# Five of the nine low one-hot rows of each counting step move from VectorE to GpSimd

## The chip, the cores and the metric

The kernel runs on one core of a Trainium2 chip. The metric is device time in microseconds, the median of several executions.

## The reference

A graph of 50,000 nodes (64 features each) and 50,000 edges, sorted by destination, goes through seven passes: a convolution, a mean aggregation, a GATv2 attention layer with four heads and batch norm, and three typed graph convolutions, each behind a layer norm and added to its input. All of them need to know how many edges leave and enter each node, which is what the first stage counts:

```python
deg = jnp.maximum(jax.ops.segment_sum(jnp.ones(dst.shape, jnp.float32), dst, num_segments=50000), 1.0)
deg_isqrt = deg ** (-0.5)
...
deg_s = jax.ops.segment_sum(ones, s, num_segments=n)
deg_r = jax.ops.segment_sum(ones, r, num_segments=n)
...
cnt = jax.ops.segment_sum(jnp.ones((edge_attr.shape[0],), x.dtype), dst0, num_segments=n)
```

## The kernel before

The program is a chain of stages, each a block in which the five engines run lists of their own, and no stage starts before all engines have left the one ahead. `prepare` (lines 131 to 403) comes first. It loads indices, x and weights, counts degrees, and makes the norms from the counts. Small planning stages follow, then the layers, which fill the rest of the run.

**The counting loop** is a histogram made by matrix products. The 392 tiles of 128 edges (50,176 slots) are taken seven at a time (`HS`), so there are 56 steps, and the loop's body holds two of them, one for each half `s` of the double-buffered tensors `hi` and `lo`. Each index is split in a low byte and a high part (`dig`, in the memory of `alpha`). For each of the seven tiles `t` of a step and both index lists `j` (0 source, 1 destination), two one-hot rows of bf16 are built on 128 partitions: `hi` with 196 columns and `lo` with 256. TensorE multiplies the two and adds up in `bank4` and `bank5`: 7 x 2 x 2 = 28 matmuls of 256 columns a step (line 390).

Three engines work on a step:

- **VectorE** (lines 322 to 332) compares `iota_b` (0..255) with the digit: one `tensor_scalar` per row, 14 `hi` rows and 9 `lo` rows (all seven of `j` = 1, and tiles 5 and 6 of `j` = 0), then adds one to `oh`.
- **ScalarE** (lines 240 to 250) makes the other five `lo` rows (`SPLIT` = 5, `j` = 0) as relu(1 - |iota - digit|): a negated copy of seven digits `low` (line 243), five `Abs` (line 246), and one `Relu` over 1280 columns (line 250), which adds one to `oh_low`.
- **TensorE** waits for `oh` and `oh_low` of the step, multiplies, and adds one to `counted`.

Before they write a half again, VectorE and ScalarE wait until `counted` shows that the step two back is done; ScalarE takes that wait only ahead of line 250. **GpSimd** makes three `iota` fills at the start of the stage (lines 261 to 263) and has nothing more in it. SyncE's queue brings x in, and copies edge attributes in HBM (line 208) behind the loop's first part. The rows of the loop lie on `iota_b`, `dig`, `hi` and `lo`, all in SBUF.

After the loop VectorE copies the counts from PSUM (line 338), TensorE turns them (line 402), and the norms are made (lines 348 to 361).

Of the kernel before, what the change touches and what calls it, by code (L numbers as in the profile page):

```python
# [4 lines left out]
P = 128  # L5
# [3 lines left out]
HS = 7  # L9
# [4 lines left out]
WT = HS + 1  # L14
WR = WT * P
SPLIT = 5
BAND = 2
FRONT = P
LN_EPS = 1e-5
# [6 lines left out]
def build_gnn(nc, a, out):  # L26
    f32, bf16, i32 = mybir.dt.float32, mybir.dt.bfloat16, mybir.dt.int32
    ALU, ACT, AX = mybir.AluOpType, mybir.ActivationFunctionType, mybir.AxisListType
# [7 lines left out]
    NS = T // HS  # L36
# [37 lines left out]
    with ctx:  # L74
# [18 lines left out]
        node_id = sb("node_id", [P, P])  # L93
        edge_id = sb("edge_id", [P, max(NS * HS * BAND, 3 * HF)])
        rel_w = sb("rel_w", [P, 2, NS * WT])
# [35 lines left out]
        def prepare():  # L131
            with nc.cleanup_on_exit(), ExitStack() as c, nc.Block() as block:
                tb = lambda name, shape, dt=f32: c.enter_context(nc.sbuf_tensor(name, shape, dt))
                sm = lambda name: nc.alloc_semaphore("pre_" + name)
# [10 lines left out]
                dig_i, dig = digits(amax).bitcast(i32), digits(alpha)  # L145
                iota_i = tb("iota_i", [P, 256], i32); iota_b = tb("iota_b", [P, 256], bf16)
                hi = tb("hi", [P, 2, 2, HS, HI], bf16)
                lo = tb("lo", [P, 2, 2, HS, 256], bf16)
# [8 lines left out]
                iotas = sm("iotas"); turned = sm("turned"); taken = sm("taken"); w_in = sm("w_in")  # L157
                x_in = sm("x_in"); oh = sm("oh"); counted = sm("counted"); hist_ok = sm("hist_ok")
                cleared = sm("cleared"); hist_t = sm("hist_t"); sq_in = sm("sq_in"); sq_out = sm("sq_out")
                oh_low = sm("oh_low"); low = tb("low", [P, 2, HS])  # L160
                dist = tb("dist", [P, SPLIT, 256], bf16)
                tails = sm("tails"); types_out = sm("types_out"); summed = sm("summed"); w_n = sm("w_n")
                x_parts = [(k * FULL // 4, (k + 1) * FULL // 4) for k in range(4)]
# [51 lines left out]
                def _(act):  # L215
# [24 lines left out]
                    def body(i, first):  # L240
                        for s in range(2):

                            A.mul(low[:, s, :], dig[:, 1, bass.ds(i * BODY + s * HS, HS)], -1.0)
                            act.drain()
                            for t in range(SPLIT):
                                A.activation(dist[:, t, :], iota_b[:, :], ACT.Abs, bias=low[:, s, t:t + 1], scale=1.0)
                            act.drain()
                            if not first:
                                act.wait_ge(counted, 2 * i + s - 1)
                            A.activation(lo[:, s, 0, 0:SPLIT, :], dist[:, :, :], ACT.Relu, bias=onesP[:, 0:1], scale=-1.0).then_inc(oh_low, 1)  # L250
                    body(0, True)
# [7 lines left out]
                @block.gpsimd  # L259
                def _(pool):  # L260
                    nc.gpsimd.iota(row_i[:, :], pattern=[[1, P]], base=0, channel_multiplier=0)
                    nc.gpsimd.iota(col_i[:, :], pattern=[[0, 1]], base=0, channel_multiplier=1)
                    nc.gpsimd.iota(iota_i[:, :], pattern=[[1, 256]], base=0, channel_multiplier=0).then_inc(iotas, 1)

                @block.vector
                def _(dve):
# [55 lines left out]
                    def body(i, first):  # L322
                        for s in range(2):
                            if not first:
                                dve.wait_ge(counted, 2 * i + s - 1)
                            for t in range(HS):
                                for j in range(2):
                                    g = i * BODY + s * HS + t
                                    ins = v.tensor_scalar(hi[:, s, j, t, :], iota_b[:, 0:HI], dig[:, 2 * j, bass.ds(g, 1)], None, ALU.is_equal)
                                    if j == 1 or t >= SPLIT:  # L330
                                        ins = v.tensor_scalar(lo[:, s, j, t, :], iota_b[:, :], dig[:, 2 * j + 1, bass.ds(g, 1)], None, ALU.is_equal)
                            ins.then_inc(oh, 1)
                    body(0, True)
                    with v.Fori(1, GI) as i:
                        body(i, False)
                    dve.wait_ge(summed, 1)
                    for j in range(2):
                        ins = v.tensor_copy(hist[:, j, :], bank[4 + j][0:R, :])
# [31 lines left out]
                @block.tensor  # L370
                def _(pe):
                    pe.wait_ge(ident_ok, 1)
                    pe.wait_ge(floats, 1)
                    pe.wait_ge(put, 1)
                    for j in range(4):
                        for b in range(NBLK):
                            ins = nc.tensor.transpose(bank[j][:, b * R:(b + 1) * R], rows[:, j, b, :], ident[0:R, 0:R])
                    ins.then_inc(turned, 1)
                    pe.wait_ge(cleared, 1)
                    for j in range(2):  # L380
                        nc.tensor.matmul(bank[4 + j][0:R, :], zb[:, 0:R], zb[:, :], start=True, stop=False)

                    def body(i, first):
                        for s in range(2):
                            pe.wait_ge(oh, 2 * i + s + 1)
                            pe.wait_ge(oh_low, 2 * i + s + 1)
                            for t in range(HS):
                                for j in range(2):
                                    for k in range(2):
                                        ins = nc.tensor.matmul(bank[4 + j][0:R, k * 256:(k + 1) * 256], hi[:, s, j, t, k * R:(k + 1) * R],  # L390
                                                               lo[:, s, j, t, :], start=False, stop=False)
                            ins.then_inc(counted, 1)
                    with nc.tensor.Fori(0, GI) as i:
                        body(i, False)
                    for j in range(2):
                        ins = nc.tensor.matmul(bank[4 + j][0:R, :], zb[:, 0:R], zb[:, :], start=False, stop=True)
                    ins.then_inc(summed, 1)
                    pe.wait_ge(hist_ok, 1)
                    for j in range(2):
                        for k in range(2):  # L400
                            for half in range(2):
                                ins = nc.tensor.transpose(bank[j][:, (2 * k + half) * R:(2 * k + half + 1) * R],
                                                          hist[:, j, k * 256 + half * P:k * 256 + (half + 1) * P], ident[0:R, 0:R])
                    ins.then_inc(hist_t, 1)
# [1200 lines left out]
        def plan():  # L1605
            with nc.cleanup_on_exit(), ExitStack() as c, nc.Block() as block:
# [36 lines left out]
                def _(dve):  # L1643
# [35 lines left out]
                    v.tensor_tensor(ahead[:, :], tot[:, 0:NS], slots(tile_at[:, 0, :])[:, :, 0], ALU.subtract)  # L1679
                    v.tensor_scalar(late[:, :], late[:, :], float(BAND * P), None, ALU.is_gt)  # L1680
                    v.tensor_scalar(early[:, :], early[:, :], float(FRONT), None, ALU.is_gt)
# [17 lines left out]
        def window_numbers():  # L1699

            with nc.cleanup_on_exit(), ExitStack() as c, nc.Block() as block:
# [26 lines left out]
                def _(dve):  # L1728
# [8 lines left out]
                    v.drain()  # L1737
                    ids = edge_id[:, 0:NS * HS * BAND].rearrange("p (n t q) -> p n t q", t=HS, q=BAND)
                    at = tile_at[:, :].rearrange("p (n t) -> p n t", t=HS)
                    for q in range(BAND):  # L1740
                        v.tensor_tensor(ids[:, :, :, q], winT[:, :, q:q + HS], at, ALU.subtract)
# [155 lines left out]
        def layer(tag, kind, table_in, table_out, k=0):  # L1897
            with nc.cleanup_on_exit(), ExitStack() as c, nc.Block() as block:
# [8 lines left out]
                msg = tb("msg", [P, 2, WT, M])  # L1907
                S = tb("S", [P, 2, BAND * HS, P])
                own = None if conv else tb("own", [P, 2, HS + 1, 2 * F if sage else F])
# [87 lines left out]
                def _(pe):  # L1997
                    def sums(j, s, first):
# [12 lines left out]
                        for b, (t0, t1) in enumerate(CH):  # L2011
                            for t in range(t0, t1):
                                col = slice((t - t0) * P, (t - t0 + 1) * P)
                                to = bank[2 * s + b][0:M, col]
                                qs = range(BAND)
                                if sage:
# [560 lines left out]
        def batch_norm(tag):  # L2577
            with nc.cleanup_on_exit(), ExitStack() as c, nc.Block() as block:
# [68 lines left out]
                def _(dve):  # L2647
# [23 lines left out]
                    body(GI - 1, False, True)  # L2671

        prepare()
        attention_weights()
        plan()
# [56 lines left out]
```

## Time and profile before

| what | value |
|---|---|
| median of 3 runs | 6772.4 us (6759.16 to 6790.24) |
| profiled execution, its own time | 6746.68 us |
| its span, first to last instruction | 6745.1 us |
| mean granted TensorE clock | 0.759 of full speed |
| PE busy | 4393.0 us (65%) |
| DVE busy | 3539.0 us (52%) |
| ACT busy | 2200.7 us (33%) |
| POOL busy | 2825.2 us (42%) |

The counting loop lies between 31 and 277 us of the span. The busy times above are sums over stages that are bound by different engines, so they say little about this loop; it is read from its own stretch. Duration and spacing differ: on VectorE one instruction's record overlaps the next one's, so the time that an instruction costs its engine is the distance between two starts, not the duration in its record.

### The profile page before, as it was taken

How to read it: one execution, taken by the hardware profiler on the slowest of the kernel's cores; microseconds unless marked ns; L12 is line 12 of the kernel's file. 1: busy time of each engine (PE TensorE's matmuls, PEld its weight loads, DVE VectorE, ACT ScalarE, POOL GpSimd, SP SyncE). 2: the span in 40 equal slices, each digit the busy share in tenths (PEclk: the TensorE clock that was granted, in tenths of full speed). 3: DMA queues.
4: the chain of work that ended last, by engine and by line, in shares of the span. 5: the costliest groups of instructions: out<-in, count | busy, mean ns of one | idle time of the engine just before them, and what ended most of it. 6: DMA issues, size and time to landing. Idle time of an engine off the chain costs nothing. (4 is left out here: it accounts for less than half of the span.)

```text
span 6745.1 us, 89039 instructions
## 1 busy us (share of the span) xinstructions
PE 4393.0 (65%) x26272; PEld 3765.7 (56%) x26272; DVE 3539.0 (52%) x9258; ACT 2200.7 (33%) x5554; POOL 2825.2 (42%) x2867
## 2 busy tenths in 40 slices
PE   6502565546666787776659999415777477757777
PEld 5402555536655454554447777315777467656677
DVE  8862555624444565665579999762323223323333
ACT  6572544513333232232225444551111111111111
POOL 0014554255543677776500000025554455545553
PEclk9855666667777787887779999656777677777777
DMA  6033666645654222222222222343444344434444
GB/s 171 6 68 82 145 144 141 134 92 126 127 116 104 63 66 66 66 68 62 50 42 55 53 52 55 81 95 80 97 93 98 69 92 96 92 81 90 96 93 91
DMA packets 1695961, 589.73 MB, mean 87 GB/s; under 512 B 1606839, under 2 KB 1626102, under 8 KB 1695498
## 3 DMA queue, kind: packets, MB, share of 16 engines
q1 hardware_dynamic: 1189958, 380.24, 25.6%
q10 hardware_dynamic: 416196, 116.81, 7.7%
q0 software_dynamic: 89600, 90.32, 6.7%
q8 instruction: 80, 1.31, 0.1%
q14 instruction: 127, 1.04, 0.0%
HBM read 378.26 MB, written 222.06 MB: 89 GB/s over the span
## 5 line engine op out<-in xcount | busy, mean ns | idle before, releaser
L1944 POOL DMA_INDIRECT early<-node_g,src_w x1176 | 1141.7, 971 | 1036.1 <-DMA edge_h<-early 583.8
L1944 POOL DMA_INDIRECT l1ring<-node_g,src_w x392 | 373.5, 953 | 444.7 <-DMA edge_h<-l1ring 243.0
L1091 POOL DMA_INDIRECT fscat<-node_g,early x392 | 439.2, 1120 | 263.5 <-issue 114.3
L1206 DVE TENSOR_TENSOR fslz<-bank,fsy 128x512 f32<-128x512 f32 x448 | 267.0, 621 | 497.6 <-issue 290.9
L1944 POOL DMA_INDIRECT l0ring<-node_g,src_w x392 | 375.4, 958 | 346.2 <-DMA edge_h<-l0ring 219.8
L2604 POOL COPY x_sb<-fbxn 128x448 f32 x56 | 31.5, 562 | 1140.0 <-DVE fbxn L2663 1140.0
L1093 POOL DMA_INDIRECT fscat<-node_g,early x392 | 433.9, 1107 | 128.2 <-issue 128.2
L1182 ACT ACTIVATE fsy<-bank 128x512 f32<-128x512 f32 x448 | 242.3, 544 | 737.1 <-remote 234.6
L2021 PE MATMUL bank<-l0S,l0msg 128*128 128x128 f32 x1568 | 297.8, 366 | 146.2 <-issue 97.6
L1141 PE MATMUL bank<-Wlr,fscatT 128*128 128x256 f32 x784 | 273.1, 433 | 171.6 <-ACT fscatT L1173 147.6
L2021 PE MATMUL bank<-l1S,l1msg 128*64 128x128 f32 x1568 | 300.6, 312 | 124.8 <-issue 124.2
L2021 PEld LDWEIGHTS bank<-l0S,l0msg 128*128 128x128 f32 x1568 | 279.8, 276 | 158.9 <-issue 153.6
L2390 PE MATMUL bank<-early,faS 128*128 128x256 f32 x1568 | 357.1, 386 | 0.0
L2390 PEld LDWEIGHTS bank<-early,faS 128*128 128x128 f32 x1568 | 296.1, 192 | 73.9 <-issue 35.2
L2021 PE MATMUL bank<-l5S,l5msg 128*128 128x128 f32 x1568 | 248.7, 323 | 123.2 <-issue 71.1
L2021 PE MATMUL bank<-l3S,l3msg 128*128 128x128 f32 x1568 | 245.0, 321 | 124.0 <-issue 79.2
L2021 PE MATMUL bank<-l4S,l4msg 128*128 128x128 f32 x1568 | 240.4, 316 | 114.5 <-issue 69.1
L2542 DVE SCALAR_TENSOR_TENSOR faagg<-bank,early,famine 128x64 f32<-128x64 f32 x1568 | 305.8, 276 | 6.2 <-ACT famine L2443 1.6
L2021 PEld LDWEIGHTS bank<-l1S,l1msg 128*64 128x64 f32 x1568 | 223.9, 161 | 150.7 <-issue 150.6
L2021 PEld LDWEIGHTS bank<-l5S,l5msg 128*128 128x128 f32 x1568 | 233.8, 236 | 130.0 <-issue 129.4
L2021 PEld LDWEIGHTS bank<-l3S,l3msg 128*128 128x128 f32 x1568 | 231.8, 234 | 128.1 <-issue 128.1
L2021 PEld LDWEIGHTS bank<-l4S,l4msg 128*128 128x128 f32 x1568 | 226.5, 229 | 120.7 <-issue 120.4
(328 smaller groups left out, 11365.2 us busy)
## 6 DMA issues: line engine op xcount, KB each, us to landing
node_g<-amax ACTq DMA_DIRECT2D x168, 224.0 KB
edge_h<-early SPq DMA_DIRECT2D x168, 224.0 KB
early<-node_g,src_w POOLq DMA_INDIRECT x1176
l0msg<-edge_a SPq DMA_DIRECT2D x56, 256.0 KB
l0msg<-edge_h SPq DMA_DIRECT2D x56, 256.0 KB
l1msg<-edge_h SPq DMA_DIRECT2D x56, 256.0 KB
alpha<-edge_h SPq DMA_DIRECT2D x56, 256.0 KB
l3win<-edge_h SPq DMA_DIRECT2D x56, 256.0 KB
```

The costliest lines, as they stand in the source:

```text
L1091: pool.indirect_dma_start(out=cat[:, s, t, 0:F], out_offset=None, in_=node_g, in_offset=bass.IndirectOffsetOnAxis(ap=src_i[:, col], axis=0 ...
L1093: pool.indirect_dma_start(out=cat[:, s, t, F:2 * F], out_offset=None, in_=node_g, in_offset=bass.IndirectOffsetOnAxis(ap=dst_i[:, col], ax ...
L1141: nc.tensor.matmul(to, catT[:, t * P:(t + 1) * P], Wlr[:, :], start=True, stop=False)
L1182: A.activation(y[:, g % 2, 0:t1 - t0, :], z_bank(g)[:, 0:(t1 - t0) * HF].rearrange("p (t c) -> p t c", c=HF), ACT.Copy, scale=SLOPE).then_ ...
L1206: v.tensor_tensor(lz[:, kind, t0:t1, :], z_bank(g)[:, 0:(t1 - t0) * HF].rearrange("p (t c) -> p t c", c=HF), y[:, g % 2, 0:t1 - t0, :], AL ...
L1944: pool.indirect_dma_start(out=ring[:, n % RING, t, :], out_offset=None, in_=table_in, in_offset=bass.IndirectOffsetOnAxis(ap=src_w[:, n * ...
L2021: ins = nc.tensor.matmul(to, msg[:, s, t + q, :], S[:, s, BAND * t + q, :], start=(q == 0 and not sage), stop=(q == BAND - 1))
L2390: ins = nc.tensor.matmul(bank[b][:, (t - t0) * HF:(t - t0 + 1) * HF], S[:, s, BAND * t + q, :], M[:, s, t + q, 0:HF], start=(q == 0), stop ...
L2542: ins = v.scalar_tensor_tensor(agg[:, s, t, h, :], bank[b][:, lo:lo + F], cc[:, 0, t, h:h + 1], mine[:, t, h, :], ALU.mult, ALU.add)
L2604: nc.gpsimd.tensor_copy(x_sb[:, bass.ds(j * BODY + s * HS, HS), :], xn[:, s, :, :]).then_inc(x_kept[s], 1)
```

## The change

GpSimd gets a list of its own in the counting loop: after the digits are there (`cleared`) it builds, for each of the 56 steps, the `lo` rows of `j` = 1 for tiles 0 to 4 (`POOLED` = 5), with the instruction that VectorE used. From step 2 on it first waits for `counted`, as the others do. It adds one to a new semaphore `oh_pool` per step, and TensorE waits for that too. VectorE builds `lo` rows only for tiles 5 and 6 of either `j`: 14 `hi` and 4 `lo` rows a step.

```diff
+POOLED = 5
...
+                    pool.wait_ge(cleared, 1)
+
+                    for n in range(NS):
+                        if n >= 2:
+                            pool.wait_ge(counted, n - 1)
+                        for t in range(POOLED):
+                            ins = nc.gpsimd.tensor_scalar(lo[:, n % 2, 1, t, :], iota_b[:, :], dig[:, 3, n * HS + t:n * HS + t + 1], None, ALU.is_equal)
+                        ins.then_inc(oh_pool, 1)
...
-                                    if j == 1 or t >= SPLIT:
+                                    if t >= (SPLIT, POOLED)[j]:
                                         ins = v.tensor_scalar(lo[:, s, j, t, :], iota_b[:, :], dig[:, 2 * j + 1, bass.ds(g, 1)], None, ALU.is_equal)
...
                             pe.wait_ge(oh_low, 2 * i + s + 1)
+                            pe.wait_ge(oh_pool, 2 * i + s + 1)
```

GpSimd's list in `prepare`, before. The rows are the three fills; what follows them is the end of the stage:

```order
L261 IOTA row_i 128x128
L262 IOTA col_i 128x1
L263 IOTA iota_i 128x256
L132 UNCONDITIONAL_BRANCH
L132 ISA [waits barrier_Pool_Activation_PE_DVE_SP_gather]
```

The same place now (nine lines further down in the file). `pre_cleared` and `pre_counted` are the semaphores `cleared` and `counted`; the last row shown is that of step 3, and the pattern goes on to step 55:

```order
L262 IOTA row_i 128x128
L263 IOTA col_i 128x1
L264 IOTA iota_i 128x256
L271 TENSOR_SCALAR lo<-iota_b,alpha 128x256 [waits pre_cleared]
L271 TENSOR_SCALAR lo<-iota_b,alpha 128x256 x9
L271 TENSOR_SCALAR lo<-iota_b,alpha 128x256 [waits pre_counted]
L271 TENSOR_SCALAR lo<-iota_b,alpha 128x256 x4
L271 TENSOR_SCALAR lo<-iota_b,alpha 128x256 [waits pre_counted]
L271 TENSOR_SCALAR lo<-iota_b,alpha 128x256 x4
```

GpSimd's list has gained 280 instructions, written out without a loop, with a wait ahead of each five.

VectorE's list at the start of a half step in the loop, before: a `hi` row of either `j` and then a `lo` row, tile by tile. The `ISA` rows compute the address of the digit:

```order
L329 ISA [waits pre_counted]
L329 TENSOR_SCALAR hi<-iota_b,alpha 128x196
L329 ISA
L329 TENSOR_SCALAR hi<-iota_b,alpha 128x196
L331 ISA
L331 TENSOR_SCALAR lo<-iota_b,alpha 128x256
L329 ISA
L329 TENSOR_SCALAR hi<-iota_b,alpha 128x196
L329 ISA
L329 TENSOR_SCALAR hi<-iota_b,alpha 128x196
L331 ISA
L331 TENSOR_SCALAR lo<-iota_b,alpha 128x256
```

And now, where the first ten rows of the step are `hi` rows and `lo` rows come with the last two tiles (here its last rows, up to the next step's wait):

```order
L338 TENSOR_SCALAR hi<-iota_b,alpha 128x196
L340 ISA
L340 TENSOR_SCALAR lo<-iota_b,alpha 128x256
L338 ISA
L338 TENSOR_SCALAR hi<-iota_b,alpha 128x196
L340 ISA
L340 TENSOR_SCALAR lo<-iota_b,alpha 128x256
L338 ISA [waits pre_counted]
```

Five `lo` rows and their address instructions have left each step of VectorE; the wait stands where it stood.

## Rows read from the trace of the kernel before

**Rows 1.** Page, busy tenths in 40 slices of 168.6 us.

```profile
PE   6502565546666787776659999415777477757777
...
DVE  8862555624444565665579999762323223323333
...
POOL 0014554255543677776500000025554455545553
PEclk9855666667777787887779999656777677777777
```

**Rows 2.** Busy time by stretch: length, then each engine's busy us.

```profile
core 0: us, PE busy (x) PEld busy (x) DVE busy (x) ACT busy (x) POOL busy (x), PEclk, DMA share, GB/s
...
31.00:277.00 246.00, 186.43 (x1572) 171.25 (x1572) 240.29 (x1289) 201.14 (x393) 0.00 (x0) 1.00 0.38 98
...
200.00:277.00 77.00, 59.09 (x506) 54.30 (x506) 73.22 (x394) 58.99 (x114) 0.00 (x0) 1.00 0.00 0
```

**Rows 3.** Groups of instructions between 31 and 277 us, shapes apart.

```profile
L329 DVE TENSOR_SCALAR hi<-iota_b,alpha 128x196 bf16<-128x196 bf16 x784 | 234.3, 527 | 1.9 <-PE bank L390 1.8
L331 DVE TENSOR_SCALAR lo<-iota_b,alpha 128x256 bf16<-128x256 bf16 x504 | 218.4, 543 | 0.0
L390 PE MATMUL bank<-lo,hi 128*98 128x256 bf16 x1568 | 184.9, 276 | 59.3 <-DVE lo L331 59.3
...
L246 ACT ACTIVATE dist<-iota_b,low 128x256 bf16<-128x256 bf16 x280 | 117.9, 497 | 3.8
L250 ACT ACTIVATE lo<-dist,onesP 128x1280 bf16<-128x1280 bf16 x56 | 76.3, 1363 | 34.4 <-PE bank L390 34.2
```

**Rows 4.** Line 329: duration ns min/median/max, first and last start.

```profile
L329 DVE TENSOR_SCALAR hi<-iota_b,alpha x784: 266/531/773, 31.1 to 272.1; 128x196 bf16<-128x196 bf16 x196
```

**Rows 5.** Timeline of VectorE inside one step: start us, us, instruction.

```profile
207.19 0.65 DVE L329 TENSOR_SCALAR hi<-iota_b,alpha 128x196 bf16<-128x196 bf16 x1
207.37 0.66 DVE L331 TENSOR_SCALAR lo<-iota_b,alpha 128x256 bf16<-128x256 bf16 x1
207.57 0.65 DVE L329 TENSOR_SCALAR hi<-iota_b,alpha 128x196 bf16<-128x196 bf16 x1
```

**Rows 6.** Timeline of TensorE, two steps of the counting loop.

```profile
204.55 3.26 PE L390 MATMUL bank<-lo,hi 128*98 128x256 bf16 x28 [1.02 <-DVE lo L331]
208.84 3.26 PE L390 MATMUL bank<-lo,hi 128*98 128x256 bf16 x28 [1.03 <-DVE lo L331]
```

**Rows 7.** Timeline of ScalarE, an early step and a late one.

```profile
42.73 0.20 ACT L243 ACTIVATE low<-alpha 128x7 f32 x1
...
45.17 1.36 ACT L250 ACTIVATE lo<-dist,onesP 128x1280 bf16<-128x1280 bf16 x1
46.44 0.19 ACT L243 ACTIVATE low<-alpha 128x7 f32 x1
...
207.85 1.36 ACT L250 ACTIVATE lo<-dist,onesP 128x1280 bf16<-128x1280 bf16 x1 [0.64 <-PE bank L390]
```

**Rows 8.** GpSimd's groups of instructions, whole run.

```profile
L2604 POOL COPY x_sb<-fbxn 128x448 f32 x56 | 31.5, 562 | 1140.0 <-DVE fbxn L2663 1140.0
...
L1629 POOL IOTA pl_tile_i<- 128x392 int32 x1 | 0.5, 455 | 308.1 <-POOLq L2250 308.1
...
L263 POOL IOTA iota_i<- 128x256 int32 x1 | 0.3, 334 | 0.0
```

**Rows 9.** Line 1091's durations; timelines of GpSimd and VectorE near 2630 us.

```profile
L1091 POOL DMA_INDIRECT fscat<-node_g,early x392: 942/947/2778, 2139.3 to 3335.7; - x196
...
2632.04 2.50 POOL L1091 DMA_INDIRECT fscat<-node_g,early  x1 [0.30 <-issue]
...
2631.69 2.02 DVE L1213 TENSOR_TENSOR fslz<-fslz,attb 128x1792 f32<-128x1792 f32 x1
```

**Rows 10.** TensorE's 28 matmuls of line 2021 at two speeds, chain that ended last.

```profile
6108.56 5.60 PE bank L2021 x28
6117.68 3.18 PE bank L2021 x28
```

More of the change, by code:

```diff
@@ L159, in prepare @@
                 cleared = sm("cleared"); hist_t = sm("hist_t"); sq_in = sm("sq_in"); sq_out = sm("sq_out")
-                oh_low = sm("oh_low"); low = tb("low", [P, 2, HS])
+                oh_low = sm("oh_low"); oh_pool = sm("oh_pool"); low = tb("low", [P, 2, HS])
                 dist = tb("dist", [P, SPLIT, 256], bf16)
```

## The prediction

> **What bounds the kernel now.** I looked first for where the change lies in the whole run. The page's slices show the counting loop in the first two of forty: VectorE 8 tenths busy, GpSimd idle, TensorE's granted clock near full [rows 1]. The stretch table says it more sharply. Between 31 and 277 us GpSimd does nothing, the granted clock is 1.00 (TensorE's upper level, 2.4 GHz), and by the last 77 us the DMA share has fallen to 0.00 [rows 2]. So the loop is not covered by a transfer, and the next stage starts only when it is over: a microsecond off or on the loop is a microsecond of the run. It is about 246 us of 6745, which caps what any edit here can bring.
>
> Next, who sets the pace inside the loop. The groups name it: TensorE was idle 59.3 us ahead of its matmuls, all of it until a VectorE `lo` row, and ScalarE 34.2 us ahead of its `Relu`, until TensorE. VectorE was idle 1.9 us in 784 instructions [rows 3]. VectorE is the bound, and the two others wait for it.
>
> What a step costs on each engine is read from distances between starts. Line 329's records grow from 266 to 773 ns in the course of the loop [rows 4] while their distance stays the same, so the duration isn't the price. On VectorE a `hi` row takes 0.18 us to the next start and a `lo` row 0.20 [rows 5]. TensorE's batches start 4.29 us apart and are 3.26 long [rows 6]. 14 x 0.18 = 2.52; the other 1.77 are nine `lo` rows at 0.197. ScalarE, on an early step where it had no wait, went from `low` to `low` in 3.71 us [rows 7]. So a step is **VectorE 4.29, ScalarE 3.71, TensorE 3.26, GpSimd 0**, and there are 56.
>
> **The change, part by part.**
>
> *Removed from VectorE:* five `lo` rows a step, 5 x 0.197 = 0.98 us, their address instructions included, since those lie inside the distances. VectorE alone would need 4.29 - 0.98 = 3.30 (3.31 before rounding). The next engine in line is ScalarE with 3.71, so the most that this part can give is 4.29 - 3.71 = 0.58 a step, 56 x 0.58 = 32.5 us. TensorE's 3.26 doesn't bind.
>
> *The added wait of TensorE* (`oh_pool`) costs nothing by itself; it is one more semaphore ahead of the same matmul. Behind it are the 28 matmuls, and for those wait all three producers through `counted`, two steps later. *GpSimd's own wait* for `counted` is late only if 5 instructions plus 3.26 us are more than two steps. Up to 1.0 us an instruction they are not. Its 280 written-out instructions and the three fills ahead of the loop [rows 8] cost nothing that I can find. No DMA is moved, and SyncE's queue has nothing to do with it.
>
> *Added on GpSimd:* five compares of 128x256 bf16 a step. No row shows one. The nearest are an `iota` of the same 256 columns, 334 ns, which reads nothing, and a copy of 128x448, 562 ns, which reads and writes but has no operand per partition [rows 8]. The dearest kind of instruction on this engine is the indirect DMA's, 947 ns when undisturbed [rows 9]. These are my ends: **0.334 and 0.947**. I take the copy's 0.562, because the compare is fewer columns but does more to each and must fetch its digit first. Five are 2.81 us a step, less than ScalarE's 3.71: if the two engines work side by side, GpSimd is not the bound.
>
> *Do they work side by side?* This decides the sign. One pair of rows speaks to it. At 2632.04 GpSimd starts an indirect DMA whose like takes 947 ns. It takes 2.50 us and ends at 2634.54. VectorE's `tensor_tensor` of line 1213, with two inputs in SBUF, ran from 2631.69 to 2633.71 [rows 9]. From that end to GpSimd's end are 0.83 us, nearly the instruction's whole length: GpSimd did not go slower beside VectorE, it stood still until VectorE was done. The loop's rows have one SBUF input, so this isn't yet the same case. But they are fast in a way that needs more than the usual way to memory. The 60 columns by which `lo` is wider than `hi` cost 0.017 us, 0.28 ns a column, while line 1213 takes 2.02 us for 1792, 1.13 ns each: four columns go through in the time of one.
>
> What the Trainium skill says is stronger than these rows. Its page "SBUF — State Buffer", section "Who interferes with whom", has a `tensor_scalar` in a 2-port mode and a GpSimd instruction exclude each other for the whole instruction. By that rule every VectorE row of this loop excludes every new GpSimd row; the trace agrees for a two-input instruction (the 2.50 us), and no run here shows it for this one.
>
> I take exclusion. Then a step is the sum of both: 3.30 + 5 x 0.562 = 6.11 us. The order of the two doesn't matter. If GpSimd gets in between VectorE's rows, VectorE is stretched; if it gets in only when VectorE has run two steps ahead and waits for `counted`, it is late by as much. The step is 6.11 - 4.29 = 1.82 longer, 56 x 1.82 = **101.9 us**. The ends give 3.30 + 1.67 = 4.97 (+38 us) and 3.30 + 4.74 = 8.04 (+210 us).
>
> Against the profiled execution's own time (6746.7, span 6745.1) that is 6848.6. It was faster than all three runs shown, and the median is 25.7 us above it; I add the 101.9 to the median, 6772.4: **6874.3 us**.
>
> **The rivals.** *B, no conflict: ScalarE becomes the bound.* The two engines work side by side, the step falls to ScalarE's 3.71, and the time is 6772.4 - 32.5 = 6739.9. For it: GpSimd's five (2.81) fit in a step, and nothing in the trace has these two forms at once. Against it: the 2.50 us. Its full gain needs a GpSimd instruction of at most 0.74 us (a fifth of 3.71), and any gain one below 0.86 (a fifth of 4.29). It ends on the other side of zero from my forecast, though by just under the 33.9 us that are 0.5%, about what a measurement of this kernel can tell from no change.
>
> *C, only the streaming part excludes.* The fixed part of a GpSimd instruction could overlap VectorE. From the `iota` of 392 and 256 columns [rows 8], (455 - 334) / 136 = 0.89 ns a column, 0.23 us for 256. The step is then 3.30 + 5 x 0.23 = 4.44, +8 us, 6781: no change that can be seen. For it: the fixed part needs no data. Against it: the blocked instruction in rows 9 needed nearly its whole length afterwards. The skill's "GPSIMD Engine Reference", section "Engine selection", calls one-input work there roughly line-rate; at its 1.2 GHz my estimate is 0.21 us for 256 columns, which would make this case +4 us. No run here shows it; the copy's 562 ns speaks against it as the whole price.
>
> *D, TensorE's clock falls.* At 6.11 us a step TensorE is busy 53% of the time. In the fifth slice it was busy 5 tenths and the granted clock was 0.6 of full [rows 1], so part of the time at the lower level, 1.2 GHz; and 28 matmuls of line 2021 took 5.60 us in one place and 3.18 in another [rows 10]. At half speed the 28 of the loop take 6.52, more than 6.11, and TensorE is the bound: +125 us, 6897. For it: those rows. Against it: a slower TensorE is busier.
>
> *E, the compare is dearer than every row,* above 0.95 us: beyond 6982, slower, whether they exclude each other or not.
>
> **How the numbers follow.** A (exclusion, 0.33 to 0.95 us) 0.62; B 0.16; C 0.12; D 0.05; E 0.05. The forecast is A's 6874.3. Slower by over 0.5% are A, D and E: 0.72. C and rather more than half of B are within 0.5%: 0.21. The rest of B is faster: 0.07. Without B the range would leave out more than it may, so it starts a little under B's number, 6736; C and A's lower part lie inside. Above it ends at 6945, which is 0.81 us an instruction, and leaves out E and the tail of A, together 0.1 to 0.15. As both signs hold most of the chance only if B and C are taken together, A's own range is worth telling: 6810 to 6945.
>
> **What the profile after would show.** TensorE's batches in the loop start about 6.1 us apart. Its idle time ahead of the matmuls ends with a GpSimd row or with a VectorE row that came late. VectorE's rows have gaps or long records where GpSimd's lie, and GpSimd's own records differ from one to the next, as the indirect DMA's did [rows 9]. ScalarE's wait for TensorE is 2 us or more a step. The loop ends near 379 us of the span instead of 277, and the rest of the run has its old lengths. A batch distance of 3.7 with ScalarE's `Relu` as the releaser would show B right and my exclusion wrong. A distance over 6 with even, undisturbed GpSimd records over 1.2 us would show E: the same sign for another reason.

## The result and the profile after

| | before | changed |
|---|---|---|
| median of 20 runs | 6751.51 us (6723.81 to 6790.24) | 6785.28 us (6750.09 to 6805.41) |
| profiled execution | 6746.68 | 6786.48 |
| span | 6745.1 | 6784.9 |
| mean granted clock | 0.759 | 0.762 |

The change made the kernel slower by a ratio of **1.0044, 95% interval [1.0026, 1.0062]**: 34 us between the medians, under the 0.5% that I had called the limit of what can be told. The forecast was +101.9.

The page of the changed kernel, busy tenths in 40 slices. Against [rows 1] the change is in GpSimd's row, 8 and 7 tenths where it had 0 and 0; the others, the granted clock too, differ by single tenths:

```profile
PE   5501556636667677776749999514777477756777
...
DVE  8862555624445456665669999772333222323333
...
POOL 8714555254443677777700000015555455545553
PEclk9955666767777788887869999756777777777778
```

The counting loop by stretch, to set beside [rows 2]. It is 275 us long and was 246. GpSimd is busy for 269.5 of it, the granted clock 0.99, so the clock did not fall:

```profile
core 0: us, PE busy (x) PEld busy (x) DVE busy (x) ACT busy (x) POOL busy (x), PEclk, DMA share, GB/s
31.00:306.00 275.00, 185.99 (x1572) 172.45 (x1572) 239.85 (x1009) 200.78 (x393) 269.52 (x280) 0.99 0.34 88
```

The groups in that stretch, beside [rows 3]. Columns: count, busy us and mean ns of one, then idle time ahead of them and what ended it.

```profile
L271 POOL TENSOR_SCALAR lo<-iota_b,alpha 128x256 bf16<-128x256 bf16 x280 | 269.6, 981 | 30.8 <-DVEq L328 29.2 <-PE bank L400 1.6
L338 DVE TENSOR_SCALAR hi<-iota_b,alpha 128x196 bf16<-128x196 bf16 x784 | 201.6, 337 | 29.7 <-PE bank L400 29.6
L400 PE MATMUL bank<-lo,hi 128*98 128x256 bf16 x1568 | 184.6, 277 | 89.0 <-POOL lo L271 51.2 <-ACT lo L251 37.7
...
L251 ACT ACTIVATE lo<-dist,onesP 128x1280 bf16<-128x1280 bf16 x56 | 76.3, 1362 | 63.0 <-PE bank L400 62.7
```

GpSimd has become the engine without idle time: its 30.8 us are 29.2 ahead of the loop and 1.6 in it. VectorE, which had been idle 1.9, is idle 29.7. TensorE's idle time went from 59.3 to 89.0 us, and is ended by GpSimd's or by ScalarE's row, no more by VectorE's. ScalarE comes last in the half of the steps because its `Relu` may start only when TensorE has finished two steps back (63.0 us idle for that, 34.4 before), and TensorE was late because of GpSimd.

Line 271 by itself, duration ns min/median/max, then first and last start:

```profile
L271 POOL TENSOR_SCALAR lo<-iota_b,alpha x280: 915/976/1142, 30.9 to 301.2; 128x256 bf16<-128x256 bf16 x140
```

Five of them make a step. TensorE's batches, 4.29 us apart in [rows 6], are now 4.90 and 4.73 in turn (start us, us):

```profile
196.30 3.23 PE L400 MATMUL bank<-lo,hi 128*98 128x256 bf16 x28 [1.51 <-ACT lo L251]
201.20 3.23 PE L400 MATMUL bank<-lo,hi 128*98 128x256 bf16 x28 [1.68 <-POOL lo L271]
205.93 3.23 PE L400 MATMUL bank<-lo,hi 128*98 128x256 bf16 x28 [1.50 <-ACT lo L251]
```

The loop's end on TensorE. The two matmuls that close the sums (line 396 before, 406 now) started, before, at 276.20:

```profile
276.20 0.59 PE L396 MATMUL bank<-zeros_w 128*98 128x512 bf16 x2
```

and now, behind the last batch, at 305.35:

```profile
302.29 3.23 PE L400 MATMUL bank<-lo,hi 128*98 128x256 bf16 x28 [1.44 <-POOL lo L271]
305.35 0.59 PE L406 MATMUL bank<-zeros_w 128*98 128x512 bf16 x2
```

That is 29.15 us later, and the next stages' first matmul comes 29.14 later (339.01 for 309.87). So the loop accounts for the whole ratio (29.15 of 6751.5 is 0.43%). The profiled executions are 39.8 us apart; the other 10.6 lie in stages that the change doesn't touch and that scatter from run to run.

### The profile page after: what moved, and what is told of

It is laid out like the page before. It is cut to its first block and busy times, and to the rows that moved or that the text cites. A ratio compares the mean times of both kernels' runs of the same rounds, so it can differ in the third digit from the quotient of the medians.

```text
span 6784.9 us, 88769 instructions
## 1 busy us (share of the span) xinstructions
PE 4409.5 (65%) x26272; PEld 3774.3 (56%) x26272; DVE 3539.5 (52%) x8978; ACT 2201.3 (32%) x5554; POOL 3090.9 (46%) x3147
## 5 line engine op out<-in xcount | busy, mean ns | idle before, releaser
L1139 PE MATMUL bank<-Wself,fsselfT 128*128 128x256 f32 x784 | 289.9, 453 | 0.0
```

Of the source, the lines that this page charges most:

```text
L1139: ins = nc.tensor.matmul(to, selfT[:, s, t * P:(t + 1) * P], Wself[:, :], start=False, stop=True)
```

## The experiments

All kernels were read in the same way: the start of TensorE's sixth batch (the 28 matmuls of a step) and of its last, 50 steps apart, and the end of that last batch.

| kernel | rows on GpSimd | 6th batch | 56th batch | us a step | loop's end |
|---|---|---|---|---|---|
| before | 0 | 58.88 | 273.10 | 4.284 | 276.36 |
| changed | 5 | 61.30 | 302.29 | 4.820 | 305.52 |
| changed, second run (`a2_after`) | 5 | 60.80 | 302.40 | 4.832 | 305.62 |
| `e1_gpsimd_alone` | 5, VectorE 1 in all | 60.37 | 285.11 | 4.495 | 288.34 |
| `e2_gpsimd_one_row` | 1, four left out | 56.30 | 241.08 | 3.696 | 244.31 |
| `e3_pooled4` | 4 | 60.73 | 278.74 | 4.360 | 282.00 |
| `e4_pooled2` | 2 | 61.03 | 282.02 | 4.420 | 285.28 |
| `e5_half_columns` | 5, half of each left out | 56.15 | 240.87 | 3.694 | 244.10 |
| `e8_scalar_six` | 0 | 57.50 | 274.88 | 4.348 | 278.11 |
| `e9_two_rows_halves` | 2, in 4 compares | 57.00 | 268.25 | 4.225 | 271.51 |
| `e10_two_rows_quarters` | 2, in 8 compares | 59.45 | 266.37 | 4.138 | 269.60 |
| `e11_halves_timed` | as `e9` | 57.45 | 268.70 | 4.225 | 271.96 |
| `e12_quarters_timed` | as `e10` | 58.69 | 265.08 | 4.128 | 268.31 |

The runs fell on several chips; on two of them the kernel before takes 5645 and 5650 us (`e1`, `e2`, `e3`, `e6` and `e9`, `e10`) instead of 6707 to 6759. The counting loop hardly differs: it ended at 305.52 and 305.62 for the changed kernel, at 271.51 and 271.96 for the halves and at 269.60 and 268.31 for the quarters (of the last two pairs the first where the kernel before takes 5650 us, the second where it takes 6759). So loops are compared across chips, to 1.3 us, and whole times only within one. In the three kernels that leave rows out the spoiled counts also send the program into its other, general branch, so their whole times (15 to 16 ms) say nothing.

My first question was which of two theories holds. Theory 1: a GpSimd compare is slow by itself and stops VectorE for a small part of its time only. Theory 2: it is cheap, as forecast, and the two engines exclude each other for whole instructions.

**GpSimd with VectorE nearly silent.**

```diff
                                 dve.wait_ge(counted, 2 * i + s - 1)
+                                v.tensor_scalar(lo[:, s, 1, HS - 1, :], iota_b[:, :], dig[:, 3, ...], None, ALU.is_equal).then_inc(oh, 1)
+                                continue
```

> The changed kernel, but from the third step on VectorE builds one low row a step instead of 18 rows (14 hi, 4 lo); the others keep what steps 0 and 1 left, so the counts are not the reference's. Theory 1 (GpSimd's compare is slow by itself, about 0.90 us, as in the one place where VectorE stood idle): GpSimd's starts stay 0.90 us apart, the batches of TensorE 5 x 0.90 = 4.5 us, the loop ends near 290 us. Theory 2 (the compare is cheap, about 0.56 us, and its 0.94 to 0.98 us are waiting for VectorE's rows): 0.56 us apart, GpSimd's five are 2.8 us, ScalarE's 3.71 us sets the step and the loop ends near 243 us.

Groups, then TensorE's last batches:

```profile
L271 POOL TENSOR_SCALAR lo<-iota_b,alpha 128x256 bf16<-128x256 bf16 x280 | 252.3, 1008 | 30.9 <-DVEq L328 29.3 <-PE bank L402 1.6
L402 PE MATMUL bank<-lo,hi 128*98 128x256 bf16 x1568 | 183.5, 275 | 72.8 <-POOL lo L271 72.8
```

```profile
280.61 3.23 PE L402 MATMUL bank<-lo,hi 128*98 128x256 bf16 x28 [1.26 <-POOL lo L271]
285.11 3.23 PE L402 MATMUL bank<-lo,hi 128*98 128x256 bf16 x28 [1.27 <-POOL lo L271]
```

4.495 us a step, 0.90 us per compare, and TensorE waits for GpSimd alone. Theory 1 to the number, theory 2 is out: VectorE had one row a step left with which to exclude it, and it still took 0.90. Of the changed kernel's 4.82, then, 4.50 are GpSimd's own and 0.32 (0.065 a compare) are what VectorE's rows cost it.

**One GpSimd row beside a busy VectorE.**

```diff
-                        for t in range(POOLED):
+                        for t in range(POOLED if n < 2 else 1):
```

> The changed kernel, but from the third step on GpSimd builds one low row a step instead of five; the four others keep what steps 0 and 1 left, so the counts are not the reference's. Theory 1 (each GpSimd compare stops VectorE for some 0.22 us and no longer): VectorE needs 3.30 + 0.22 = 3.52 us, ScalarE's 3.71 sets the step, the loop ends near 243 us, and one pause of 0.2 us a step is to be seen in VectorE's starts. Theory 2 (it shuts VectorE out for its whole 0.9 us): VectorE needs 3.30 + 0.9 = 4.2 us, the step is 4.2 and the loop ends near 270 us.

```profile
L400 PE MATMUL bank<-lo,hi 128*98 128x256 bf16 x1568 | 183.6, 275 | 28.8 <-DVE lo L340 24.7 <-POOL lo L271 4.0
L338 DVE TENSOR_SCALAR hi<-iota_b,alpha 128x196 bf16<-128x196 bf16 x784 | 171.9, 285 | 7.3 <-PE bank L400 5.3
...
L251 ACT ACTIVATE lo<-dist,onesP 128x1280 bf16<-128x1280 bf16 x56 | 76.3, 1362 | 6.6 <-PE bank L400 1.1
```

3.70 us a step: ScalarE's own pace, which is seen in its `Relu` being idle only 6.6 us in the whole loop. The group's row puts TensorE's waits down to VectorE, but single steps show `Relu` last: it ended at 229.81 (228.45 + 1.36), and the batch began 0.10 later:

```profile
228.45 1.36 ACT L251 ACTIVATE lo<-dist,onesP 128x1280 bf16<-128x1280 bf16 x1
229.91 3.23 PE L400 MATMUL bank<-lo,hi 128*98 128x256 bf16 x28 [0.54 <-DVE lo L340]
```

Early in the loop ScalarE was still ahead, and the batches, at 56.30, 59.83, 63.37 and 66.89, came at VectorE's pace, 3.53 a step: its 3.30 and one pause of 0.23. With GpSimd all but out of the way, the gain that the change was computed to give is there; it is what rival B described, though with four of GpSimd's five rows left out.

**Four rows on GpSimd.**

```diff
-POOLED = 5
+POOLED = 4
```

> Four low rows on GpSimd, five on VectorE; nothing is left out. Theory 1 with pauses: GpSimd needs 4 x 0.965 = 3.86 us, VectorE 14 x 0.18 + 5 x 0.197 + 4 x 0.22 = 4.39, so VectorE sets the step again, 4.39 against 4.29 before: the loop is 5 us longer than before and 24 us shorter than with five rows, 6757 against 6752 (no difference that a run can tell). Rival (no pauses on VectorE, GpSimd alone was the bound): VectorE 3.51, the step is GpSimd's 3.86, the loop 24 us shorter than before, 6728. Rival (whole instructions exclude each other): 3.51 + 3.86 = 7.4 us a step.

```profile
L338 DVE TENSOR_SCALAR hi<-iota_b,alpha 128x196 bf16<-128x196 bf16 x784 | 209.8, 339 | 3.9 <-PE bank L400 3.7
L400 PE MATMUL bank<-lo,hi 128*98 128x256 bf16 x1568 | 187.5, 279 | 62.7 <-DVE lo L340 62.7
```

VectorE is the bound again (idle 3.9 us, and it alone ends TensorE's waits), at 4.36 us a step: it should need 2.52 + 5 x 0.197 = 3.51 for its rows, so four GpSimd rows cost it 0.85, 0.21 each. The loop ended 5.6 us later than before, 5 were expected. The ratio in 10 runs was 1.0007 [0.9997, 1.0017]; 5.6 of 5645 is 1.0010. Giving GpSimd a row saves VectorE 0.197 us and costs it 0.21.

The pauses can be seen one by one in the changed kernel. VectorE's timeline of the end of a step:

```profile
202.03 0.49 DVE L340 TENSOR_SCALAR lo<-iota_b,alpha 128x256 bf16<-128x256 bf16 x1
202.45 0.26 DVE L338 TENSOR_SCALAR hi<-iota_b,alpha 128x196 bf16<-128x196 bf16 x1
202.62 0.41 DVE L340 TENSOR_SCALAR lo<-iota_b,alpha 128x256 bf16<-128x256 bf16 x1
202.82 0.27 DVE L338 TENSOR_SCALAR hi<-iota_b,alpha 128x196 bf16<-128x196 bf16 x1
203.01 0.49 DVE L340 TENSOR_SCALAR lo<-iota_b,alpha 128x256 bf16<-128x256 bf16 x1
203.42 0.26 DVE L338 TENSOR_SCALAR hi<-iota_b,alpha 128x196 bf16<-128x196 bf16 x1
```

and GpSimd's compares in the same place; each row merges two, so that three of them started at 201.98, 202.94 and 203.91:

```profile
201.98 1.95 POOL L271 TENSOR_SCALAR lo<-iota_b,alpha 128x256 bf16<-128x256 bf16 x2
...
202.94 1.89 POOL L271 TENSOR_SCALAR lo<-iota_b,alpha 128x256 bf16<-128x256 bf16 x2
```

The `lo` row that started at 202.03 is followed after 0.42 us, the one at 203.01 after 0.41, where [rows 5] have 0.20; the rows between keep 0.17 to 0.20. One pause of 0.2 us comes with each of these GpSimd compares, in the VectorE row that starts 0.05 to 0.07 us after it. The compare of 203.91 falls in the stretch where VectorE is idle anyway (to 204.58). The rest of the compare's 0.96 us runs beside VectorE.

**What a compare costs with VectorE idle,** by a probe ahead of the loop.

```diff
...
+                    for cols_ in (256, 256, 128, 64):
+                        nc.gpsimd.tensor_scalar(probe[:, at:at + cols_], iota_b[:, 0:cols_], col_f[:, 0:1], None, ALU.is_equal)
+                        at += cols_
+                    nc.gpsimd.tensor_copy(probe[:, at:at + 256], iota_b[:, :])
```

> The changed kernel with five more GpSimd instructions near 5 us of the span, where VectorE is idle until 12 us: compares of 256, 256, 128 and 64 columns, bf16 to bf16, with a per-partition scalar, then a copy of 256 columns. Nothing is left out and the end should not move. Theory 1: the compare of 256 costs 0.9 us start to start with VectorE idle, and the price goes with the columns or is a fixed part, which the 128 and the 64 tell: if it is all columns, 0.45 and 0.23; if a fixed part of 0.12 as the iotas have it, 0.51 and 0.32. Theory 2: 0.56 for 256 columns. The copy of 256 about 0.40 (from the 562 ns of 448 columns) in either.

```profile
L269 POOL TENSOR_SCALAR probe<-iota_b,col_f 128x256 bf16<-128x256 bf16 x2 | 1.9, 928 | 3.5 <-DVE ident L302 3.5
L269 POOL TENSOR_SCALAR probe<-iota_b,col_f 128x128 bf16<-128x128 bf16 x1 | 0.6, 590 | 0.0
L269 POOL TENSOR_SCALAR probe<-iota_b,col_f 128x64 bf16<-128x64 bf16 x1 | 0.4, 430 | 0.0
L271 POOL COPY probe<-iota_b 128x256 bf16<-128x256 bf16 x1 | 0.4, 386 | 0.0
```

```profile
6.16 1.50 POOL L269 TENSOR_SCALAR probe<-iota_b,col_f 128x256 bf16<-128x256 bf16 x2
...
7.06 1.01 POOL L269 TENSOR_SCALAR probe<-iota_b,col_f 128x128 bf16<-128x128 bf16 x2
8.02 0.39 POOL L271 COPY probe<-iota_b 128x256 bf16<-128x256 bf16 x1
```

The second compare of 256 starts at 6.16, the one of 128 at 7.06, the copy at 8.02. So 256 columns cost 0.90 us from start to start, and the 1.01 us row holds the compares of 128 and 64 together. By the durations 256 to 128 columns are (928 - 590) / 128 = 2.6 ns a column. The **copy of the same 256 columns took 386 ns, the compare 928**. Here lies the error of my price. The one run of this kernel took 5670.63 us, 25 more than the kernel before on that chip (5645.32).

**Is it one pause per compare, whatever its size?** Two rows on GpSimd, and five half rows:

```diff
-POOLED = 5
+POOLED = 2
```

> Two low rows on GpSimd, seven on VectorE; nothing is left out. From four rows (4.347 us a step measured) the pause is (4.347 - 2.52 - 5 x 0.197) / 4 = 0.21 us a GpSimd row. Theory 1 (a row given to GpSimd saves VectorE 0.197 and costs it 0.21, whatever their number): 2.52 + 7 x 0.197 + 2 x 0.21 = 4.32 us a step, the loop 2 us longer than before. Rival (the pauses of four rows come of the two running in step and are fewer with two rows): 2.52 + 7 x 0.197 = 3.90, the loop 22 us shorter.

```profile
L338 DVE TENSOR_SCALAR hi<-iota_b,alpha 128x196 bf16<-128x196 bf16 x784 | 195.8, 308 | 3.6 <-PE bank L400 3.4
```

4.42, not 4.32. The rival's shorter loop is out, but my number missed too: VectorE (3.6 us idle, so still the bound) lost 4.42 - 3.90 = 0.52 for two compares, 0.26 each, more than the 0.21 with four. Its starts show where the rest went. Beside the compare that ran from 152.86 to 154.01, the `lo` row of 153.03 is followed after 0.40, as before, but the `hi` row of 153.81 is held up too: the next starts at 154.06, after 0.25 us instead of 0.18. So there are two pauses here, of 0.20 and some 0.06 us.

```diff
-                            ins = nc.gpsimd.tensor_scalar(lo[:, n % 2, 1, t, :], iota_b[:, :], ...
+                            W_ = 256 if n < 2 else 128
+                            ins = nc.gpsimd.tensor_scalar(lo[:, n % 2, 1, t, 0:W_], iota_b[:, 0:W_], ...
```

> The changed kernel, but from the third step on GpSimd's five compares take 128 of 256 columns; the other halves keep what steps 0 and 1 left, so the counts are not the reference's, and only the counting loop is to be read. GpSimd: 0.577 us for 128 columns in the probe, with VectorE beside it some 0.64, 3.2 a step, no longer the bound. Theory 1 (VectorE is stopped while GpSimd's columns go through, so half the columns are half the pause): 3.30 + 5 x 0.11 = 3.85 us a step on VectorE, just over ScalarE's 3.71. Rival (the pause is one fixed handing over, whatever the columns): 3.30 + 5 x 0.21 = 4.35 a step.

```profile
L272 POOL TENSOR_SCALAR lo<-iota_b,alpha 128x128 bf16<-128x128 bf16 x270 | 196.0, 743 | 4.1 <-PE bank L401 2.6
L401 PE MATMUL bank<-lo,hi 128*98 128x256 bf16 x1568 | 183.4, 275 | 28.9 <-ACT lo L251 14.4 <-POOL lo L272 11.7 <-DVE lo L341 2.7
L339 DVE TENSOR_SCALAR hi<-iota_b,alpha 128x196 bf16<-128x196 bf16 x783 | 173.9, 289 | 4.1 <-PE bank L401 2.4
```

3.69 us a step, under my 3.85 and far from the fixed pause's 4.35. ScalarE, with its 3.71, hardly waited (`Relu` idle 6.6 us), so VectorE lost at most (3.69 - 3.30) / 5 = 0.08 us a compare, a third of what 256 columns cost. GpSimd's records, on the other hand, were longer than expected, 743 ns in the mean against 590 alone.

**Smaller pieces, then.** If half a compare takes less than half from VectorE, a whole row in pieces is cheaper than VectorE's own 0.197. Two rows on GpSimd, in 4 compares of 128 or 8 of 64 columns, nothing left out:

```diff
-POOLED = 5
+POOLED = 2
...
+                            for c in range(0, 256, 128):
+                                ins = nc.gpsimd.tensor_scalar(lo[:, n % 2, 1, t, c:c + 128], iota_b[:, c:c + 128], ...
```

> Two low rows a step on GpSimd, each as two compares of 128 columns; VectorE has seven low rows; nothing is left out. With half columns VectorE was never idle at 3.69 us a step, so a compare of 128 cost it (3.69 - 3.30) / 5 = 0.08 us at most; with two whole rows a compare of 256 cost it (4.42 - 3.90) / 2 = 0.26. Theory 1a (what a compare takes from VectorE grows faster than its columns): 3.90 + 4 x 0.08 = 4.22 us a step, the loop 4 us shorter than before. Rival (it goes by columns in total, 0.26 for 256 in whatever pieces): 3.90 + 0.52 = 4.42, as with whole rows.

```profile
268.25 3.26 PE L401 MATMUL bank<-lo,hi 128*98 128x256 bf16 x28 [0.79 <-DVE lo L341]
```

> The same two rows in four compares of 64 columns each, eight a step, 0.38 us each in the probe and so 3.1 us of GpSimd. Theory 1a: VectorE loses at most 0.04 a compare, 3.90 + 8 x 0.04 = 4.22 or less. Rival (by columns in total): 4.42. Rival (a fixed part for each compare, 0.08 as for the halves): 3.90 + 8 x 0.08 = 4.54.

```profile
L272 POOL TENSOR_SCALAR lo<-iota_b,alpha 128x64 bf16<-128x64 bf16 x448 | 231.7, 585 | 32.8 <-DVEq L329 29.2 <-PE bank L401 3.4
L401 PE MATMUL bank<-lo,hi 128*98 128x256 bf16 x1568 | 184.0, 276 | 53.7 <-POOL lo L272 41.3 <-DVE lo L341 10.8 <-ACT lo L251 1.5
L339 DVE TENSOR_SCALAR hi<-iota_b,alpha 128x196 bf16<-128x196 bf16 x784 | 179.5, 269 | 6.5 <-PE bank L401 6.3
```

The halves came out at 4.225 (4.22 expected), the quarters at 4.14: two same rows, the same columns, 4.42 whole, 4.23 in halves, 4.14 in quarters. "By columns in total" is refuted. With the quarters GpSimd comes last for most of TensorE's waits (41.3 of 53.7 us), and VectorE is idle for 6.5: GpSimd's eight compares are the bound, 0.52 us each in the mean where 0.38 were expected.

The quarters' starts show that either engine can be the one that is held up. Near 153 us GpSimd's compares start 0.43 apart, and each costs a VectorE row 0.06 (0.24 to the next start instead of 0.18):

```profile
152.92 0.48 POOL L272 TENSOR_SCALAR lo<-iota_b,alpha 128x64 bf16<-128x64 bf16 x1
...
153.00 0.32 DVE L339 TENSOR_SCALAR hi<-iota_b,alpha 128x196 bf16<-128x196 bf16 x1
153.24 0.28 DVE L341 TENSOR_SCALAR lo<-iota_b,alpha 128x256 bf16<-128x256 bf16 x1
```

Near 223 us the compares start 0.56 apart, and VectorE's rows keep their 0.18 and 0.20 without any pause:

```profile
222.92 0.64 POOL L272 TENSOR_SCALAR lo<-iota_b,alpha 128x64 bf16<-128x64 bf16 x1
...
223.19 0.28 DVE L341 TENSOR_SCALAR lo<-iota_b,alpha 128x256 bf16<-128x256 bf16 x1
223.39 0.26 DVE L339 TENSOR_SCALAR hi<-iota_b,alpha 128x196 bf16<-128x196 bf16 x1
```

With the halves GpSimd's compares start 0.80 to 0.84 apart for 0.58 in the probe (149.87, 150.67, 151.51 us). So smaller pieces take less from VectorE in part because GpSimd does more of the waiting. What decides which of the two waits was not tried.

The loops of halves and quarters are shorter than both kernels': by 4.9 and 6.8 us than the loop before, by 34 and 36 us than the changed one. They were timed:

> The kernel with two rows on GpSimd in halves, timed. Its loop was 4.9 us shorter than the loop before (271.5 against 276.4 us at its end). Theory 1 (the loop is all that differs): 4.9 of 5645 or 6707 us, a ratio of 0.9991 to 0.9993; with an interval of some 0.1 to 0.2% that may not be told from 1. Rival (VectorE and GpSimd left something behind for the next stages): above 1.000.

> The kernel with two rows on GpSimd in quarters, timed. Its loop ended 6.8 us earlier than the loop before (269.6 against 276.4). Theory 1: a ratio of 0.9988 to 0.9990, again near what the runs can tell from 1. Rival: above 1.000.

Ratios 0.9997 [0.9976, 1.0018] and 0.9987 [0.9963, 1.0011]; the loops ended at 271.96 and 268.31 us. The loops repeat, to 0.5 and 1.3 us. In the whole time the gain is within what can't be told from none.

**Moving work to ScalarE instead,** from the kernel before: the digits negated once ahead of the loop, six rows on ScalarE, eight on VectorE.

```diff
-SPLIT = 5
+SPLIT = 6
...
+                    A.mul(low[:, :], dig[:, 1, :], -1.0)
...
-                            A.mul(low[:, s, :], dig[:, 1, bass.ds(i * BODY + s * HS, HS)], -1.0)
```

> The kernel before, not the changed one: GpSimd stays out; ScalarE makes the negated digits once ahead of the loop (0.26 us a step less) and takes six low rows instead of five, VectorE eight instead of nine. VectorE 14 x 0.18 + 8 x 0.197 = 4.10, ScalarE 6 x 0.42 + 0.1 + 1.48 + 0.05 = 4.15: a step of 4.15 against 4.285, the loop 7.6 us shorter, ratio 0.9987. Rival (the digit's address, now computed in the loop, and the drain ahead of each step cost ScalarE what the hoisting saves): 4.4 or more, slower by 6 us.

```profile
151.34 1.57 ACT L249 ACTIVATE lo<-dist,onesP 128x1536 bf16<-128x1536 bf16 x1
153.08 2.50 ACT L245 ACTIVATE dist<-iota_b,low 128x256 bf16<-128x256 bf16 x6 [0.16 <-issue]
```

4.35 us a step instead of 4.15, the loop 1.8 us longer than before, the ratio 0.9983 [0.9965, 1.0001], which these 2 us can't have made. ScalarE was the bound. From the `Relu`'s end (151.34 + 1.57) to the next `Abs` are 0.17 us. They were 0.17 before too, from the end at 46.53 (45.17 + 1.36, [rows 7]) to an `Abs` that the trace has at 46.70, with `low` started at 46.44 in between: the small instruction lay in a gap that is there without it, and taking it out saved nothing. One more `Abs` (0.42) and a `Relu` longer by 0.21 then make 3.71 into 4.34. The rival was right in kind; whether the drain makes the gap was not tried.

**The changed kernel again:**

> The changed kernel as it is, timed against the kernel before on the chip of these runs, where the kernel before takes 5645 us and scatters less. Theory 1 (only the counting loop differs, by the 29.15 us between the two profiles): 5645 + 29 = 5674, a ratio of 1.0052. Rival (a part of the 34 us between the first medians came from later stages): a ratio above 1.006.

The run did not fall on the chip that was meant: 6722.69 against 6706.97, ratio 1.0029 [1.0011, 1.0046]. It holds the loop's share, 29.26 us or 1.0044. The rival's 34 us would be 1.0051 here, outside it.

## Why the prediction was wrong

The time lies in the range and the sign was right, but the rise was a third of the forecast and its mechanism another. Both were luck. The range holds 6785.28 because it was stretched down to 6736 for rival B; the forecast's own, 6810 to 6945, does not. The sign I had from an exclusion that did not happen; it came out the same by a price that I had too low. Of the signs that I named, GpSimd's rows do end TensorE's waits and VectorE does pause beside them, but the sizes are others: the batches are 4.82 us apart and not 6.1, the loop ends at 305.5 and not near 379, ScalarE waits 1.1 us a step and not 2.

- **The loop lies open, a microsecond there is a microsecond of the run: right.** 29.15 us on the loop, 1.0044 on the whole.
- **VectorE gives up five `lo` rows and would then need 3.30; ScalarE's 3.71 is next: right.** With one GpSimd row left the step was 3.70.
- **The step that failed first: "I take exclusion. Then a step is the sum of both".** The sum would be 6.11; the step took 4.82. What the runs show is the larger of two lists: GpSimd's own five compares, and VectorE's rows plus a short pause for each compare. VectorE lost 0.20 to 0.26 us for a compare (0.26 with two rows, in two pauses, 0.21 with four, 0.2 in the changed kernel's timeline), not the whole 0.96. The 2.50 us record of [rows 9] looks like a true wait: another of the same line ran from 2626.13 to 2627.98 and ended 0.81 after the VectorE instruction of line 1213 ahead of it. But it was an indirect DMA behind one long two-input instruction. I carried it over to rows that are 0.18 us apart, and from the GpSimd side, which waited, to the VectorE side, which I made wait. The Trainium skill's rule ("SBUF — State Buffer", section "Who interferes with whom": the one that comes first holds the shared ports for its whole instruction and the other blocks) does not hold for this pair in these runs: of a 0.96 us GpSimd compare VectorE lost about a fifth, and GpSimd lost 0.065 of it to VectorE's rows. That they conflict at all, the trace confirms.
- **The second failed step: "I take the copy's 0.562".** The compare costs 0.90 us alone and 0.96 beside VectorE; a copy of the same shape 0.386. It is a term taken from the wrong row: near in shape and engine, but another operation. My upper end, 0.947, was close by luck: it is the record of an indirect DMA. The two errors had opposite signs. With the measured 0.96 my exclusion would have given 3.30 + 4.82 = 8.1 us a step, +215 us; with my 0.562 and no exclusion I would have had the gain of rival B.
- **Rival B** named the right boundary and I passed over it: above 0.86 us an instruction (a fifth of 4.29) the change loses even without a conflict. The instruction takes 0.96, the step is 5 x 0.964 = 4.82, and 56 x (4.82 - 4.284) = 30 us.
- **Rival C** had the size of the exclusion for whole rows, 0.23 us a compare for 0.2 to 0.26 measured, but not its law, as the halves show (0.08), and the wrong price beside it. VectorE's list would be 3.30 + 5 x 0.21 = 4.35 us; GpSimd's 4.82 hides it. The Trainium skill's "roughly line-rate" ("GPSIMD Engine Reference", section "Engine selection"), by my estimate 0.21 us for 256 columns, is wrong for this compare by a factor of four: 0.90.
- **Rival D (clock): no.** 0.99 in the stretch. **Rival E (dear beyond every row): nearly;** 0.96 against its 0.95, but it put the time above 6982 because it kept the sum.
- **The chances.** 0.72 went to slower by over 0.5%. All of it hung on exclusion or on a compare still dearer; the measured ratio, 1.0044, falls in the 0.21 for no change. The case that happened, no full exclusion and GpSimd itself the bound, had no line of its own.

Why no number of whole rows helps is then plain. With n whole rows on GpSimd, VectorE needs 4.29 - 0.197 n and 0.21 to 0.26 n more for pauses, and GpSimd 0.96 n: measured 4.28, 4.42, 4.36 and 4.82 for 0, 2, 4 and 5. One and three whole rows, with nothing left out, were not run.

## What to carry to other kernels

Price a moved instruction on its new engine by the same operation there, not by the nearest shape; where the trace has none, the first question is at which price that engine becomes the bound (here 4.29 / 5 = 0.86 us), and it deserves a case of its own. Work given to GpSimd to relieve VectorE is paid back in pauses: here 0.197 us saved and 0.21 to 0.26 lost for each row. If GpSimd has time to spare, cutting its instructions in smaller pieces took less from VectorE for the same columns (4.42, 4.23, 4.14 us a step), at the cost of more GpSimd time (busy 2.1, 3.2 and 4.1 us a step for the same two rows). The two gains in the loop, 5 and 7 us, did not show in the whole time.

## What the runs showed of the hardware that I had not expected

- GpSimd's compare of bf16 with a per-partition scalar costs 2.6 ns a column between 128 and 256 columns; a copy of 256 columns is 386 ns in all.
- Its effect on VectorE, per compare, was 0.21 to 0.26 us for 256 columns, 0.08 for 128 ((4.225 - 3.90) / 4, with VectorE idle 1.2 us in the loop) and, for 64, 0.06 or nothing, and so not proportional. With 256 columns there is a pause of 0.2 us near the compare's start, with two rows a step a second one of 0.06. What VectorE is spared GpSimd loses in part: its compares of 128 columns start 0.80 to 0.84 us apart beside VectorE for 0.58 alone, those of 64 columns 0.43 to 0.56 for 0.38. Which part of the instruction makes a pause was not tried.
- VectorE's records for the same row grew through the loop before (266 to 773 ns) at an unchanged distance. With GpSimd beside it they stayed short (337 ns in the mean against 527), while the engine got less done; but they stayed short without GpSimd too, with eight `lo` rows and VectorE not the bound (264 ns, `e8_scalar_six`). A record's duration is no measure of an engine's load; what makes it grow is open.
